# A gated scan and a ternary MLP: the upper half of the hidden rows is turned by VectorE and DRAM instead of by TensorE

## What is computed

```python
h = nan_to_num(take(embed_table, x, axis=0))            # 16384 rows of 256
xn = layernorm(h)
f, i = sigmoid(xn @ Wf.T), sigmoid(xn @ Wi.T)
g = where(c >= 0, c + 0.5, sigmoid(c))                  # c = xn @ Wh.T; the reference does this in logs
s[t] = f[t] * s[t - 1] + i[t] * g[t],  s[-1] = 0.5      # a scan along each sequence
h = h + s
xn = layernorm(h)
r = maximum(bitlinear(xn, w_fc) + gate * (xn @ v.T @ fast_b.T @ u.T), 0)
out = h + bitlinear(r * r, w_proj)                      # bitlinear: ternary weights with a scale per row
```

## Time and profile before

| | us |
|---|---|
| median of three runs | 915.22 |
| profiled execution, device time | 913.92 |
| its span | 912.1 |
| TensorE busy | 880.3 (97%) |
| ScalarE busy | 788.5 (86%) |
| VectorE busy | 755.8 (83%) |
| GpSimd busy | 418.5 (46%) |
| granted TensorE clock | 0.998 of full |

### The profile page before, as it was taken

How to read it: one execution, slowest core, us unless ns; L and a number is a source line. 1 busy time by engine, 2 the same in 40 slices (tenths; PEclk the granted TensorE clock), 3 DMA queues, 4 the chain that set the end, 5 groups by cost and what they waited for, 6 DMA issues and landing times.

```text
span 912.1 us, 18335 instructions
## 1 busy us (share of the span) xinstructions
PE 880.3 (97%) x5505; PEld 482.1 (53%) x5505; DVE 755.8 (83%) x1338; ACT 788.5 (86%) x1195; POOL 418.5 (46%) x457
## 2 busy tenths in 40 slices
PE   4979999999999999999999999999999999999997
PEld 2435554555555455555455555545555545555554
DVE  6988888788888888888888888888888888888766
ACT  5677998888998888998888899888889988899884
POOL 7446544445544445554444554444555444433110
PEclk9999999999999999999999999999999999999999
DMA  4123434432333443333443233344333334423311
GB/s 146 24 53 68 92 73 87 99 78 69 89 82 75 98 98 61 79 85 74 91 98 78 68 88 82 75 97 98 63 81 89 73 85 97 97 51 82 78 47 47
DMA packets 225372, 72.88 MB, mean 80 GB/s; under 512 B 200134, under 2 KB 220176, under 8 KB 225344
## 3 DMA queue, kind: packets, MB, share of 16 engines
q1 hardware_dynamic: 219200, 68.33, 33.8%
q0 software_dynamic: 6144, 4.21, 2.0%
HBM read 27.68 MB, written 24.64 MB: 57 GB/s over the span
## 4 chain that ended last, share of the span: by engine, by line
PE 85%; DVE 4%; ACT 4%; issue 2%; DMA 2%; SPq 1%; POOL 1%; ACTq 0%; POOLq 0%; DVEq 0%
PE bank L848 33%; PE bank L870 22%; PE y_ps L784 22%; PE bank L884 3%; PE turned L824 1%; ACT sq L584 1%; PE turned L761 1%; ACT normed L509 1%; ACT relu L571 1%; SPq L338 1%; DMA x_cols<-x_rows 1%; PE turned L772 1%; PE turned L771 1%; DMA spill<-hid_blocks 1%; DVE hid L1277 0%
## 5 line engine op out<-in xcount | busy, mean ns | idle before, releaser
L870 PE MATMUL bank<-x_cols,fc_t 128*128 128x512 f16 x1024 | 244.1, 381 | 3.6 <-ACT relu L571 3.6
L420 POOL TENSOR_SCALAR var_eps<-moments 128x4 f32<-128x4 f32 x64 | 59.5, 929 | 387.9 <-DVE moments L1020 387.6
L848 PE MATMUL bank<-x_cols,w_hi 128*128 128x512 f16 x768 | 229.8, 381 | 4.9 <-ACT forget L560 2.0
L848 PE MATMUL bank<-x_cols,w_lo 128*128 128x512 f16 x768 | 229.4, 380 | 0.0
L784 PE MATMUL y_ps<-proj_t,sq_hi 128*128 128x256 bf16 x1024 | 225.6, 273 | 3.0 <-DVE sq_lo L1203 3.0
L784 PE MATMUL y_ps<-proj_t,sq_lo 128*128 128x256 bf16 x1024 | 225.6, 273 | 0.0
L571 ACT ACTIVATE relu<-bank,relu_scale 128x512 f32<-128x512 f32 x256 | 159.3, 689 | 39.6 <-PE bank L884 39.0
L410 POOL DMA_INDIRECT rows_raw<-table,idx_now x128 | 148.0, 1156 | 59.9 <-issue 30.8
L870 PEld LDWEIGHTS bank<-x_cols,fc_t 128*128 128x128 bf16 x1024 | 95.0, 98 | 130.8 <-issue 28.3
L1203 DVE TENSOR_TENSOR sq_lo<-sq,sq_hi 128x1024 f16<-128x1024 f32 x128 | 150.6, 1214 | 5.8 <-ACT sq L584 5.7
L509 ACT ACTIVATE normed<-h,shift,rstd 128x256 f32<-128x256 f32 x256 | 132.7, 601 | 5.4 <-POOL shift L428 5.4
(11 more groups left out here) (143 smaller groups left out, 919.7 us busy)
## 6 DMA issues: line engine op xcount, KB each, us to landing
out<-out_sb SPq DMA_DIRECT2D x31, 512.0 KB, 3.0
spill<-hid_blocks SPq DMA_DIRECT2D x30, 256.0 KB, 2.1
hid_rows<-spill SPq DMA_DIRECT2D x120, 64.0 KB
rows_raw<-table,idx_now POOLq DMA_INDIRECT x128, 2.6
x_cols<-x_rows SPq DMA_TRANSPOSE x120, 3.6
sq<-w_fc SPq DMA_DIRECT2D x1, 1024.0 KB, 5.5
pj_raw<-w_proj SPq DMA_DIRECT2D x1, 1024.0 KB, 4.8
out<-out_sb SPq DMA_DIRECT2D x2, 256.0 KB, 2.1
```

The lines of the kernel that those rows point to most:

```text
L848: ins = pe.matmul(gate_bank(p, par)[:, :], w[:, k, q, :], x_part(0, par, part)[:, :, k, :], start=(k == 0 and w is w_hi and part == 0), st ...
L870: ins = pe.matmul(fc_bank(f, par)[:, :], fc_t[:, f, k, :], x_part(1, 0, part)[:, :, k, :], start=(opens and k == 0 and part == 0), stop=(n ...
```

## The change

In the loop both halves now go through 32x32 blocks and DRAM. `hid_blocks`, `hid_rows` and the DRAM buffer get a place for each half. `turn_blocks` writes its blocks in another order, so that what `fetch_rows` reads is contiguous over 128 numbers, 512 bytes. TensorE turns the upper half only in the last step (and both halves in steps 0 and 1). The residual sum is made by halves, with the statistics of each half behind it (`measure_half`); `sum_up` joins them, and also does for the second layer norm the two small operations that GpSimd did in `root`. `w_raw`, used at the start alone, lies in `relu`. The diff, without its declarations of semaphores and its calls in the steps that are written out by hand:

```diff
-        stats = [sb(f"stats{k}", [P, TILES, 6]) for k in range(2)]
+        stats = [sb("stats0", [P, TILES, 6]), sb("stats1", [P, TILES, KD, 6])]
...
-        hid_blocks = sb("hid_blocks", [P, CHUNK])
-        hid_rows = sb("hid_rows", [P, TILES, P])
+        hid_blocks = sb("hid_blocks", [P, KD, CHUNK])
+        hid_rows = sb("hid_rows", [P, KD, CHUNK])
...
-        w_raw = sb("w_raw", [P, 6, D])
+        w_raw = relu[:, 0:2, :, :].rearrange("p a b (c d) -> p (a b c) d", d=D)[:, 0:6, :]
...
-            def spill_blocks(c):
-                sp.wait_ge(blocks_ready, c - 1)
+            def spill_blocks(c, e):
+                sp.wait_ge(blocks_ready[e], c - 1)
                 pass_on(sp, sp_passed, c)
-                sp.dma_start(spill[:, :], hid_blocks[:, :]).then_inc(blocks_spilled, 16)
-            def fetch_rows(c, par):
-                sp.wait_ge(blocks_spilled, 16 * (c - 1))
+                sp.dma_start(spill[e, :, :], hid_blocks[:, e, :]).then_inc(blocks_spilled[e], 16)
+            def fetch_rows(c, e):
+                sp.wait_ge(blocks_spilled[e], 16 * (c - 1))
                 pass_on(sp, sp_passed, c)
-                rows = spill.rearrange("(i t) (j q c) -> i t j q c", t=BLOCK, j=TILES, q=B)
+                rows = spill[e, :, :].rearrange("(i t) (q x) -> i q t x", t=BLOCK, q=B)
                 for i in range(B):
-                    sp.dma_start(hid_rows[:, :, BLOCK * i:BLOCK * (i + 1)],
-                                 rows[i].rearrange("t j q c -> q t j c")).then_inc(blocks_moved[par], 16)
+                    sp.dma_start(hid_rows[:, e, i * P:(i + 1) * P], rows[i]).then_inc(blocks_moved[e], 16)
...
-                    spill_blocks(n)
-                    fetch_rows(n, par)
+                    spill_blocks(n, 0)
+                    fetch_rows(n, 0)
                 if known_below(n, N - 1):
                     wait(sp, gate_done, 6 * n)
                     pass_on(sp, sp_passed, n)
                     turn_rows(0, n + 1, 1 - par)
+                    spill_blocks(n, 1)
+                    fetch_rows(n, 1)
...
-                pool.wait_ge(moments_ready[k], TILES * (c + 1))
                 wait(pool, normed_ready[k], TILES * c)
-                pass_on(pool, pool_passed, c)
-                pool.tensor_scalar(var_eps[k][:, :], moments[k][:, :, 1], EPS, None, ALU.add)\
-                    .then_inc(var_ready[k], 1)
-                pool.tensor_scalar(minus_mean[k][:, :], moments[k][:, :, 0], -1.0, None, ALU.mult)\
-                    .then_inc(var_ready[k], 1)
+                if k == 0:
+                    pool.wait_ge(moments_ready[k], TILES * (c + 1))
+                    pass_on(pool, pool_passed, c)
+                    pool.tensor_scalar(var_eps[k][:, :], moments[k][:, :, 1], EPS, None, ALU.add)\
+                        .then_inc(var_ready[k], 1)
+                    pool.tensor_scalar(minus_mean[k][:, :], moments[k][:, :, 0], -1.0, None, ALU.mult)\
+                        .then_inc(var_ready[k], 1)
                 pool.wait_ge(var_ready[k], 2 * c + 2)
+                if k == 1:
+                    pass_on(pool, pool_passed, c)
                 pool.tensor_tensor(rstd[k][:, :], var_eps[k][:, :], minus_half[:, :], ALU.pow)\
...
                 wide(4, True)
-                if front and not first:
+                if isinstance(n, int) and n == N - 1:
                     turn_upper(n)
...
+            def measure_half(c, rows, e):
+                for j in range(TILES):
+                    dve.bn_stats(stats[1][:, j, e, :], rows[:, j, e * P:(e + 1) * P]).then_inc(stats_ready[1], 1)
+            def sum_up(c):
+                dve.wait_ge(stats_ready[1], TILES * KD * (c + 1))
+                wait(dve, var_ready[1], 2 * c)
+                pass_on(dve, dve_passed, c)
+                for j in range(TILES):
+                    dve.bn_aggr(moments[1][:, j, :], stats[1][:, j, :, :].rearrange("p e s -> p (e s)"))\
+                        .then_inc(moments_ready[1], 1)
+                dve.wait_ge(moments_ready[1], TILES * (c + 1))
+                wait(dve, rstd_ready[1], c)
+                dve.tensor_scalar(var_eps[1][:, :], moments[1][:, :, 1], EPS, None, ALU.add).then_inc(var_ready[1], 1)
+                dve.tensor_scalar(minus_mean[1][:, :], moments[1][:, :, 0], -1.0, None, ALU.mult).then_inc(var_ready[1], 1)
...
-                    if e == 0 and steady:
-                        dve.wait_ge(blocks_ready, n - 2)
+                    if steady:
+                        dve.wait_ge(blocks_ready[e], n - 2)
...
-                def residual(c, at):
-                    if late:
-                        dve.wait_ge(blocks_moved[par], 16 * B * h)
-                        dve.wait_ge(out_ready, c - 1)
-                        dve.tensor_tensor(h1[:, at, :, 0:P], hid_rows[:, :, :], h0[:, at, :, 0:P], ALU.add)\
-                            .then_inc(h1_low, 1)
-                        dve.wait_ge(hid_turned, c + 1)
-                        dve.tensor_tensor(h1[:, at, :, P:D], turned_half, h0[:, at, :, P:D], ALU.add)\
-                            .then_inc(h1_ready, 1)
-                        dve.wait_ge(h1_low, c - 1)
+                def turn_blocks(e):
+                    dve.wait_ge(scanned, 4 * n + 2 * e + 2)
+                    wait(dve, blocks_spilled[e], 16 * (n - 2))
+                    dve.transpose(hid_blocks[:, e, :].rearrange("p (q j c) -> p j q c", q=B, j=TILES),
+                                  hid[:, e, :].rearrange("p (j q c) -> p j q c", q=B, j=TILES)).then_inc(blocks_ready[e], 1)
+                def residual_whole(c, at):
+                    dve.wait_ge(hid_turned, c + 1)
+                    dve.tensor_tensor(h1[:, at, :, :], turned_rows, h0[:, at, :, :], ALU.add).then_inc(h1_ready, 1)
+                    dve.wait_ge(h1_ready, c + 1)
+                    for e in range(KD):
+                        measure_half(c, h1[:, at, :, :], e)
+                    sum_up(c)
+                def residual_half(c, at, e, summed):
+                    over = lambda rows: rows[:, at, :, e * P:(e + 1) * P].rearrange("p j (i c) -> p j i c", c=BLOCK)
+                    dve.wait_ge(blocks_moved[e], 16 * B * (c - 1))
+                    dve.tensor_tensor(over(h1), hid_rows[:, e, :].rearrange("p (i j c) -> p j i c", i=B, j=TILES),
+                                      over(h0), ALU.add).then_inc(summed, 1)
+                def residual_low(c, at):
+                    dve.wait_ge(out_ready, c - 1)
+                    residual_half(c, at, 0, h1_low)
+                    dve.wait_ge(h1_low, c - 1)
+                    measure_half(c, h1[:, at, :, :], 0)
+                def residual_high(c, at):
+                    if isinstance(c, int) and c == N - 1:
+                        dve.wait_ge(hid_turned, KD + 1)
+                        dve.tensor_tensor(h1[:, at, :, P:D], turned_half, h0[:, at, :, P:D], ALU.add).then_inc(h1_ready, 1)
                     else:
-                        dve.wait_ge(hid_turned, c + 1)
-                        dve.tensor_tensor(h1[:, at, :, :], turned_rows, h0[:, at, :, :], ALU.add).then_inc(h1_ready, 1)
+                        residual_half(c, at, 1, h1_ready)
                     dve.wait_ge(h1_ready, c + 1)
-                    measure(1, c, h1[:, at, :, :])
+                    measure_half(c, h1[:, at, :, :], 1)
+                    sum_up(c)
...
-                    turn_blocks()
+                    turn_blocks(0)
...
                     scan(1)
+                if known_below(n, N - 1):
+                    turn_blocks(1)
                 emit(n - 2, h - 1, par)
                 if known_below(n, N - 2):
                     guard(n + 2, 64 * (h + 1 + par), par)
                 if front:
-                    residual(n, par)
+                    residual_low(n, par)
+                    residual_high(n, par)
                 if known_below(n, N - 2):
                     guard_sum(n + 2, par)
...
-    spill = nc.dram_tensor("spill", (P, CHUNK), F32, kind="Internal").ap()
+    spill = nc.dram_tensor("spill", (KD, P, CHUNK), F32, kind="Internal").ap()
```

More of the change, by code:

```diff
@@ L215, in build @@
         hid_turned = sem("hid_turned")
-        blocks_ready = sem("blocks_ready")
-        blocks_spilled = sem("blocks_spilled")
-        blocks_moved = [sem("blocks_moved_even"), sem("blocks_moved_odd")]
+        blocks_ready = [sem("blocks_ready0"), sem("blocks_ready1")]
+        blocks_spilled = [sem("blocks_spilled0"), sem("blocks_spilled1")]
+        blocks_moved = [sem("blocks_moved0"), sem("blocks_moved1")]
         h1_low = sem("h1_low")
@@ L1011, in guard_sum, with measure @@
                                          ALU.min, ALU.max).then_inc(h0_ready, 1)
-            def measure(k, c, rows):
+            def measure(c, rows):
                 for j in range(TILES):
-                    dve.bn_stats(stats[k][:, j, :], rows[:, j, :]).then_inc(stats_ready[k], 1)
-                dve.wait_ge(stats_ready[k], TILES * (c + 1))
```

(12 more changed lines are left out.)

6 lines of the change are left out of this document (1 added, 5 removed).

## The result

The changed kernel takes 1112.05 us, median of 4 runs (1109.69 to 1116.14); the kernel before took 915.22 (912.91 to 915.28) in 4 runs beside it. The ratio is 1.216, 95% interval 1.213 to 1.220. It is slower, as forecast, but by 197 us instead of 127, and above the upper end of the range, 1075.

A forecast was written before the change was run, and what follows sets the result against it. TensorE, busy throughout the 26.90 us step, was taken as the bound. The new chain, 25.86 + L = 31.3 us a step, adds 3.6 us once and 4.4 in 28 steps: +127, 1042 us; range 1020 to 1070, 8 in 10 1000 to 1075.

The forecast's parts named there:

- `project` to the end of gate 5: First link of the loop step's chain, on TensorE: claimed unchanged at 12.60 us.
- to the end of the upper scan: Link from the end of gate 5 to the end of VectorE's upper scan: claimed unchanged at 4.83 us.
- transpose: New transpose of the upper half on VectorE: 0.84 us, as for the lower half, 0.2 more as the bound.
- spill: New spill of the upper half, from transpose to first fetch issue: 2.23 us, bound 0 to 0.9 more for the queue.
- fetch, L: Upper half's new fetch, first issue until VectorE goes on: 5.4 us, 3.0 of it data; bounds 3.5 and 7.24.
- residual to `project`: From upper residual sum through statistics by halves, L1010 and first `sq_lo` to TensorE's start: 2.46 + 2.30 + 0.1 us.
- second stall: Inside `project`, TensorE's third part waits for VectorE's third `sq_lo`: 0.5 us a step.
- Taking four engines: In the new fetch, the four values of `q` give four DMA engines at 22 GB/s each, 88 GB/s: 3.0 us.
- what stands around the data: The part of L that is not data, from step 2's fetch: 7.24 less 4.80 us.
- All 16 engines at full rate: Rival for the fetch with runs of 512 bytes: L 3.5 us, step 29.4, total 985 us; chance 0.12.
- The one in which the longer runs give nothing: Rival: fetch bound by its four issues or latency; L 7.24 us, step 33.1, total 1094 us; chance 0.08.
- The other sign: Rival: spill and fetch hidden by VectorE's work, TensorE gains 0.44 us in each of 29 steps; 902 us, chance 0.02.

The follow-up runs named there:

- The run with the wait filled: The changed kernel, but TensorE runs 20 products of 512 columns, whose result nobody reads, ahead of each `project`; 1055.44 us.
- the run by `q`: The changed kernel, but its four fetches are cut by `q` instead of by `i`, slowest dimension 32 instead of 4, same bytes and runs; 987.39 us.

## Why the prediction was wrong

The sign and the mechanism were right, the time was not. One step of the changed kernel, from the `project` at 512.95 to that at 547.41, is 34.46 us, and falls into the terms of the sum so:

| term | forecast | measured |
|---|---|---|
| `project` to the end of gate 5 | 12.60 | 527.97 - 512.95 = 15.02 |
| to the end of the upper scan | 4.83 | 4.91 |
| transpose | 0.84 | 533.64 - 532.88 = 0.76 |
| spill | 2.23 | 535.88 - 533.64 = 2.24 |
| fetch, L | 5.4 | 542.52 - 535.88 = 6.64 |
| residual to `project` | 2.46 + 2.30 + 0.1 = 4.86 | 547.41 - 542.52 = 4.89 |
| second stall | 0.5 | 0 |

The transpose ends at 532.92 + 0.72 = 533.64. The two ends that no chain row has are these, gate 5's on TensorE and the scan's on VectorE (531.61 + 1.27 = 532.88):

```profile
527.97 0.38 PE L775 MATMUL turned<-part_hi,spread 128*128 128x512 f16 x1
```

```profile
531.61 1.27 DVE L1299 TENSOR_TENSOR_SCAN hid<-forget,value 128x256 f32<-128x256 f32 x2
```

- **The step that failed** is "`project` to the end of gate 5: 12.60 us on TensorE, unchanged". The duration came from a row at 2.4 GHz, and the same sum put a wait of some 5 us just ahead of it. Behind this wait the clock is at 1.2 GHz for 5 us: +2.4 in this step, less the second stall of 0.5 that it swallows. The run with the wait filled gives the net price, 1.96 us a step, 55 us in all. No rival held it either. The trace of before did show it, in a stretch that I hadn't looked at: TensorE waits 2.29 us at the start of the program, and then the clock is at half:

```profile
53.01 0.62 PE L761 MATMUL turned<-x_cols,low_a 128*32 128x512 f16 x4 [2.29 <-DVE x_cols L1035]
53.56 3.03 PE L870 MATMUL bank<-x_cols,fc_t 128*128 128x512 f16 x8
...
56.86 1.89 PE L870 MATMUL bank<-x_cols,fc_t 128*128 128x512 f16 x8
```

```profile
53.00:54.00 1.00, 0.99 (x6) 0.28 (x7) 0.00 (x0) 0.32 (x1) 0.92 (x3) 0.50 0.00 0
54.00:55.00 1.00, 1.00 (x4) 0.41 (x3) 0.69 (x2) 0.28 (x1) 0.83 (x2) 0.50 0.00 0
```

  The same eight products take 3.03 us and then 1.89. A mean clock of 0.998 over the span hid it.
- **L was mis-sized.** The mean wait at the second residual sum is 5.17 us, and begins 0.97 us after the first issue (542.52 - 5.67 - 535.88), so L is 6.1 us on the mean, against 5.4. Taking four engines was right. Their rate, 18 to 19 GB/s and not the 22 that the sum took from a spill and a store, which write to DRAM, makes the data 0.7 longer; what stands around the data is 0.6 shorter than the 2.44 taken from step 2; and the output's store, which stood behind the fetch in the same queue and which the sum did not price, costs 0.5 to 0.6. 28 x 0.7 = 20 us.
- **The rest of the links held** within 0.1 us: the transpose, the spill, the residual with its statistics by halves. As forecast the four issues take 2.21 us instead of 4.17, so the spill isn't late, and ScalarE and the transposing DMA of `x_cols` weren't waited for.
- **The rivals.** All 16 engines at full rate fell, because the order of `q` had not changed; the run by `q` then came to the L of that rival, 3.3 for 3.5, and its time, 987 for 985 us. But it did so at 132 GB/s and a share of 0.45, with 1.9 us of data for the rival's 1.1 and 1.3 around them for 2.44: the two errors cancel, which is luck. The one in which the longer runs give nothing came near the measured time, 1094, but for another reason: its L of 7.24 isn't there. The other sign needed L under 0.6.

Per step, 1.96 + 0.7 makes 2.7 us too little in the sum, where 33.67 - 31.3 = 2.4 are found. The remainder of 0.3 us, some 8 us in all, stays open; the steps differ among themselves by more, and the last of the 28 waits only 2.97 us.

## What to carry to other kernels

When a change makes TensorE wait, the work behind the wait must be priced at the clock that it will have there, and here a stretch at the start of the trace of before showed that price. Before a transfer is put into a chain, look at the share of the DMA engines and not only at GB/s: 0.24 to 0.34 went with a slowest dimension of 4, and turning the loops around made it 2.8 us shorter at the same bytes and runs, part of that by getting clear of the store. And what waits first in an in-order queue delays all that stands behind it: moving one wait behind two operations that don't need it gave back 103 us of 197, half of it because TensorE, waiting less at a time, kept its clock.

## What the runs showed of the hardware

- Behind each of the changed kernel's 29 waits at the start of `project`, 2.97 to 5.90 us, the granted clock is 0.50 for 2.6 to 5.9 us, while TensorE is busy without a break; a product of 256 columns then comes every 0.213 us instead of 0.109. In the run by `q` there are 28 such waits of 1.6 to 2.9 us, and the clock stayed at 1.00 behind 21 of them; behind the other seven, and behind one of 2.29 us in the kernel before, it was at 0.50, in five cases only from 1.0 us or more after TensorE had begun.
- A fetch whose slowest dimension is 4 ran at 71 to 77 GB/s, a share of 0.24 to 0.27, with runs of 512 bytes, and at 55 GB/s and 0.34 with runs of 128 bytes. With 32 there, L fell from 6.1 to 3.3 us, at 132 GB/s and a share of 0.45. The rule that the prediction cites, from the Trainium skill, "DMA: Bandwidth & Descriptors", section "Why a DMA increments its semaphore by 16 and not by 1", on how many engines a DMA is spread over gives 4 and 16 here; the small packets, 4 and 16 for each DMA, agree with both.
- The issue of a fetch DMA takes 0.51 to 0.55 us cut by `i` and 0.43 cut by `q`, that of a spill 0.33 to 0.34.
